# Cross-attention and expert layer on one core: second half ranked on shifted logits beside the exponentials, weight rows split behind their transposition, first-layer weights split in three portions

## The reference

```python
x = x + _L0_xattn_ref(_layernorm(x), ctx_768, Wq, Wk, Wv, Wo, bo)   # 8 heads of 64
x = x + _L0_ffn_ref(_layernorm(x), router_w, ...)

router_logits = flat @ router_w + router_b            # 1024 tokens x 8 experts
router_probs = jax.nn.softmax(router_logits, axis=-1)
topk_probs, topk_idx = jax.lax.top_k(router_probs, 2)
weights = jnp.zeros_like(router_probs).at[jnp.arange(T)[:, None], topk_idx].add(topk_probs)
shared_out = gelu(flat @ sw1 + sb1) @ sw2 + sb2
h1 = gelu(jnp.einsum('td,edh->teh', flat, rw1) + rb1)  # every expert, 256 wide
expert_out = jnp.einsum('teh,ehd->ted', h1, rw2) + rb2
mixed = jnp.einsum('ted,te->td', expert_out, weights)
```

## Time and profile before

| | |
|---|---|
| device time, median of 3 runs | 435.71 us (435.40 to 437.55) |
| device time of the profiled execution | 435.49 us |
| span of its profile | 433.7 us |
| mean granted TensorE clock | 0.992 of full |
| busy: PE / PEld / DVE | 420.8 / 327.0 / 278.3 us |
| busy: ACT / POOL | 219.3 / 257.8 us |
| chain that ended last: PE / POOL / DVE / ACT | 83% / 8% / 3% / 2% |

### The profile page before, as it was taken

One profiled execution on the slowest core, in us unless ns is written; L12 is line 12 of the kernel. 1 busy time (PEld: TensorE's weight loads), 2 busy tenths in 40 slices (PEclk: granted clock), 3 DMA queues, 4 the chain that ended last, 5 costly groups with the idle time before them and its releaser, 6 DMA issues.

```text
span 433.7 us, 7166 instructions
## 1 busy us (share of the span) xinstructions
PE 420.8 (97%) x2500; PEld 327.0 (75%) x2500; DVE 278.3 (64%) x553; ACT 219.3 (51%) x384; POOL 257.8 (59%) x176
## 2 busy tenths in 40 slices
PE   8999999999999999999999999999999999878997
PEld 6787777786877877777878786778686776756896
DVE  4785858785546858673458596743495865656553
ACT  3555353342763534336735353447244754883783
POOL 4628995868474849382757483917352900873981
PEclk9999999999999999999999999999999999997999
DMA  7400002000000020000000300000000032003200
GB/s 227 139 1 2 0 2 59 0 2 0 2 0 2 2 58 2 0 2 0 2 2 0 110 2 2 2 1 0 2 2 2 2 97 79 19 1 112 85 26 24
DMA packets 16329, 11.59 MB, mean 27 GB/s; under 512 B 9580, under 2 KB 13208, under 8 KB 16296
## 3 DMA queue, kind: packets, MB, share of 16 engines
q1 hardware_dynamic: 16296, 11.15, 9.5%
HBM read 10.55 MB, written 0.56 MB: 26 GB/s over the span
## 4 chain that ended last, share of the span: by engine, by line
PE 83%; POOL 8%; DVE 3%; ACT 2%; issue 1%; DMA 1%; SPq 1%; POOLq 0%; ACTq 0%
PE ps L1254 19%; PE ps L1238 10%; PE ps L1174 10%; PE ps L1239 10%; PE ps L1240 10%; PE ps L1086 7%; PE ps L1088 7%; PE ps L1087 7%; POOL work L559 4%; PE ps L1128 2%; PE ps L1186 1%; POOL g_lo L773 1%; DMA probs<-in_L_xattn_Wv_dram 1%; POOL w_lo L757 1%; POOL work L557 1%
## 5 line engine op out<-in xcount | busy, mean ns | idle before, releaser
L849 ACT ACTIVATE probs<-ps 128x512 f32<-128x512 f32 (+1 forms) x208 | 123.8, 598 | 134.8 <-PE ps L1240 127.8
L970 DVE TENSOR_REDUCE maxes<-ps 128x1 f32<-128x402 f32 x256 | 131.6, 567 | 55.4 <-PE ps L1174 55.3
L559 POOL TENSOR_TENSOR work<-work,probs 128x1024 f32<-128x1024 f32 x54 | 128.9, 2388 | 15.9 <-ACT probs L849 13.0
L1254 PE MATMUL ps<-probs,v_sb 128*64 128x256 f32 (+1 forms) x832 | 93.4, 381 | 0.0
L1254 PEld LDWEIGHTS ps<-probs,v_sb 128*64 128x64 f32 (+1 forms) x832 | 58.3, 137 | 33.9 <-ACT probs L849 3.7
L1238 PE MATMUL ps<-g_hi,ctxT_hi 97*128 97x512 f32 (+1 forms) x208 | 82.9, 399 | 0.0
L557 POOL TENSOR_TENSOR work<-probs 128x1024 f32<-128x1024 f32 x14 | 33.5, 2392 | 82.0 <-issue 61.6
L1239 PE MATMUL ps<-g_lo,ctxT_hi 96*128 96x512 f32 (+1 forms) x208 | 82.0, 394 | 0.0
L1240 PE MATMUL ps<-g_hi,ctxT_lo 96*128 96x512 f32 (+1 forms) x208 | 81.7, 393 | 0.0
L1174 PE MATMUL ps<-ctxT_hi,g_hi 96*128 96x402 f32 x256 | 72.6, 356 | 0.7 <-ACT ctxT_hi L788 0.4
L773 POOL TENSOR_TENSOR g_lo<-probs,g_hi 128x512 fp32r<-128x512 f32 x32 | 40.5, 1290 | 35.1 <-ACT g_hi L871 35.1
(11 more groups left out here) (147 smaller groups left out, 526.4 us busy)
## 6 DMA issues: line engine op xcount, KB each, us to landing
v_sb<-weight_rows SPq DMA_DIRECT2D x12, 256.0 KB, 4.0
raw<-in_ctx_T_dram SPq DMA_DIRECT2D x3, 600.4 KB, 4.5
work<-in_L_ffn_rw_dram SPq DMA_DIRECT2D x1, 1024.0 KB, 7.5
raw<-weight_rows SPq DMA_DIRECT2D x4, 256.0 KB, 3.6
g_hi<-neg_row SPq DMA_DIRECT2D x60, 0.5 KB, 2.0
raw<-in_ctx_T_dram SPq DMA_DIRECT2D x3, 150.8 KB, 2.8
x_sb<-in_x_dram SPq DMA_DIRECT2D x1, 384.0 KB, 5.6
early<-in_WqkT_dram SPq DMA_DIRECT2D x1, 336.0 KB, 5.1
```

The costliest lines, as they stand in the source:

```text
L559: ops.tensor_tensor(acc, acc, pr, ALU.add).then_inc(summed, 1)
L849: nc.scalar.activation(probs[0:rows, n % SLOTS, j, :], s_bank(chunk_no(*w))[0:rows, :], ACT.Exp, scale=SCALE).then_inc(probs_ready, 1)
L970: v.tensor_reduce(maxes[:, p % 2, i * T + t, blk:blk + 1], src[:, 0:BW], AX.X, ALU.max).then_inc(ring_taken, 1)
L1254: ins = mm(o_bank[DH * i:DH * (i + 1), :], v_sb[0:rows, c, h * DH:(h + 1) * DH], probs[0:rows, n % SLOTS, j, i * S:(i + 1) * S], start=(c ...
```

## The change

- `plan_experts`: "xt" goes from turn 4 to turn 5, "router" and "exp" from turn 5 to turn 6, "rank" behind the seconds of turn 6, "wrow" behind the seconds of turn 7. The step "best" is gone in both halves.
- Ranking no longer waits for exponentials: `mark_best` finds the two largest of the shifted logits (maximum 0; filler 1.0) and makes a mask of them. In the last half it follows the router directly on DVE; in the first half it stays at "rank". Then, with the exponentials: masked product, sum, reciprocal, and one product that writes the weights in all four row groups of `wrow`.
- Both halves now subtract the maximum on DVE and take one exponential instruction. In the last half exponentials and masked ones lie in PSUM (bank `O_BANK`).
- The split into high and low part of the weight rows is made after the transposition: `wT` gets the rounded copy, and eight of its rows then the difference (one more DVE instruction).
- First-layer weights are split in portions of 3, 2 and 4 experts, after pairs (0, 0), (0, 2) and (0, 3); the bias addition on POOL moves from after (0, 3) to after (0, 2), before the second portion. The quotients of (0, 0), (0, 2) and (1, 0) wait for them.
- Start: ACT casts Wv after all four context blocks, POOL takes two low parts before that of Wv.

```diff
@@ plan @@
-              (n_units + 1, 3): [("rank",), ("best",)], (3, 6): [("ring", ("wrow",))]}
+              (n_units + 1, 3): [("rank",)], (3, 6): [("ring", ("wrow",))]}
-        main += [("w1", k) for k in range(2) if n == 2 * k] + followers(n, n_units)
+        main += [("w1", k) for k, at in enumerate((0, 2, 3)) if n == at] + followers(n, n_units)
@@ plan_experts @@
-    amid = {0: [("sums", last_pair), ("quotient", last_pair + (0,)), ("quotient", last_pair + (1,))], 2: [("ring", ("y", b))], 4: [("ring", ("xt", b))],
-            5: [("ring", ("router", last)), ("exp", last)], 6: [("rank", last), ("best", last)], 7: [("ring", ("wrow", last))]}
-    behind = {2: [("roots", b)], 3: [("norm", b)]}
+    amid = {0: [("sums", last_pair), ("quotient", last_pair + (0,)), ("quotient", last_pair + (1,))], 2: [("ring", ("y", b))], 5: [("ring", ("xt", b))],
+            6: [("ring", ("router", last)), ("exp", last)]}
+    behind = {2: [("roots", b)], 3: [("norm", b)], 6: [("rank", last)], 7: [("ring", ("wrow", last))]}
@@ build @@
-    W1_CUT = NE - PAIRS
+    W1_PARTS = (slice(0, PAIRS - 1), slice(PAIRS - 1, PAIRS + 1), slice(PAIRS + 1, NE))
+        lexp_bank, chosen_bank = (ps[:, O_BANK, i * TH * E:(i + 1) * TH * E].rearrange("p (t e) -> p t e", e=E)
+                                  for i in range(2))
+        def routing(w):
+            return (lexp_bank, chosen_bank) if w == NHALF - 1 else (lexp[:], chosen[:])
@@ gpsimd @@
             low_part(0, 0)
+            low_part(0, 1)
...
-            for i in range(1, BLOCKS):
+            for i in range(2, BLOCKS):
...
-            g.memset(rprob[:], -1.0).then_inc(consts_ready, 1)
+            g.memset(logit[:], 1.0).then_inc(consts_ready, 1)
...
-                if kind == "scores" and w == (0, 3, NU - 1, 0):
-
-                    added(0, 3)
+                if kind == "w1" and w == 1:
+
+                    added(0, 2)
...
-                    es = (slice(0, W1_CUT), slice(W1_CUT, NE))[w]
+                    es = W1_PARTS[w]
-                    added(0, 2 * w)
+                    added(0, (0, 2, 3)[w])
@@ scalar @@
             for i in range(BLOCKS):
                 high_part(0, i)
-                if i == 1:
-                    act.wait_ge(s_wv, 16)
-                    nc.scalar.copy(wv_hi[:], wv_sb).then_inc(wv_hi_ready, 1)
+            act.wait_ge(s_wv, 16)
+            nc.scalar.copy(wv_hi[:], wv_sb).then_inc(wv_hi_ready, 1)
...
+                    nc.scalar.activation(routing(w)[0], logit[:, :, 0:E], ACT.Exp).then_inc(lexp_ready, 1)
@@ vector @@
-                if p == 0 and b < 2:
-                    dve.wait_ge(w1_split, b + 1)
+                if (b, p) in ((0, 0), (0, 2), (1, 0)):
+                    dve.wait_ge(w1_split, ((0, 0), (0, 2), (1, 0)).index((b, p)) + 1)
+            def mark_best(w):
+                dve.wait_ge(logit_ready, w + 1)
+                for t in range(TH):
+                    ins = v.max(top8[:, t, :], logit[:, t, 0:E])
+                then_own(ins)
+                then_own(v.memset(top8[:, :, TOP:8], 1.0))
+                for t in range(TH):
+                    ins = v.match_replace(low[:, t, 0:E + 8 - TOP], top8[:, t, :], logit[:, t, 0:E + 8 - TOP], 1.0)
+                then_own(ins)
+                then_own(v.tensor_scalar(mask[:], low[:, :, 0:E], 0.5, None, ALU.is_gt))
...
+                        then_own(v.tensor_reduce(neg_lmax[:], lg, AX.X, ALU.max, negate=True))
+                        v.tensor_tensor(lg, lg, neg_lmax[:].unsqueeze(2).to_broadcast([P, TH, E]), ALU.add
+                        if b == NHALF - 1:
+                            mark_best(b)
...
-                        v.tensor_copy(wT[:, b * HALF:(b + 1) * HALF], src).then_inc(ring_taken, 1)
+                        cols = slice(b * HALF, (b + 1) * HALF)
+                        then_own(v.tensor_copy(wT[:, cols], src))
+                        v.tensor_tensor(wT[WLO:WLO + E, cols], src[WLO:WLO + E, :], wT[WLO:WLO + E, cols].bitcast(F32),
+                                        ALU.subtract).then_inc(ring_taken, 1)
                 elif kind == "rank":
+                    le, ch = routing(w)
+                    if w < NHALF - 1:
+                        mark_best(w)
                     dve.wait_ge(lexp_ready, w + 1)
+                    v.tensor_tensor(ch, le, mask[:], ALU.mult)
+                    then_own(v.tensor_reduce(lsum[:], le, AX.X, ALU.add))
                     then_own(v.reciprocal(rsum[:], lsum[:]))
...
+                    v.tensor_tensor(wr, ch.unsqueeze(2).to_broadcast([P, TH, P // WLO, E]),
+                                    rsum[:].unsqueeze(2).unsqueeze(3).to_broadcast([P, TH, P // WLO, E]), ALU.mult
+                                    ).then_inc(w_ready, 1)
```

More of the change, by code:

```diff
@@ L380, in build @@
         w_rows = sb("w_rows", [P, NHALF, HALF])
-        logit = sb("logit", [P, TH, E])
+        logit = sb("logit", [P, TH, E + 8])
+        mask = sb("mask", [P, TH, E])
         neg_lmax = sb("neg_lmax", [P, TH])
@@ L852, in _ @@
                     act.wait_ge(logit_ready, w + 1)
-                    if w == NHALF - 1:
-                        nc.scalar.activation(lexp[:], logit[:], ACT.Exp).then_inc(lexp_ready, 1)
-                        continue
-                    for t in range(TH):
-                        ins = nc.scalar.activation(lexp[:, t, :], logit[:, t, :], ACT.Exp,
-                                                   bias=neg_lmax[:, t:t + 1])
-                    ins.then_inc(lexp_ready, 1)
+                    nc.scalar.activation(routing(w)[0], logit[:, :, 0:E], ACT.Exp).then_inc(lexp_ready, 1)
                 elif kind == "split":
@@ L1017, in _ @@
+                    if w < NHALF - 1:
+                        mark_best(w)
                     dve.wait_ge(lexp_ready, w + 1)
-                    then_own(v.tensor_reduce(lsum[:], lexp[:], AX.X, ALU.add))
+                    v.tensor_tensor(ch, le, mask[:], ALU.mult)
+                    then_own(v.tensor_reduce(lsum[:], le, AX.X, ALU.add))
                     then_own(v.reciprocal(rsum[:], lsum[:]))
                     if w == 0:
-                        dve.wait_ge(consts_ready, 3)
-                    else:
-                        dve.wait_ge(w_ready, w)
@@ L1025, in _ @@
-                    then_own(v.tensor_tensor(rprob[:, :, 0:E], lexp[:], rsum[:].unsqueeze(2).to_broadcast([P, TH, E]),
-                                             ALU.mult))
-                    for t in range(TH):
-                        ins = v.max(top8[:, t, :], rprob[:, t, 0:E])
-                    then_own(ins)
-                    then_own(v.memset(top8[:, :, TOP:8], -1.0))
-                    for t in range(TH):
-                        ins = v.match_replace(low[:, t, 0:E + 8 - TOP], top8[:, t, :], rprob[:, t, 0:E + 8 - TOP], 0.0)
@@ L1033, in _ @@
-                    ins.then_inc(ranked, 1)
-                elif kind == "best" and w == NHALF - 1:
-                    dve.wait_ge(ranked, w + 1)
-                    dve.wait_ge(wrow_zero, 2)
-                    wr = wrow[:, w * TH:(w + 1) * TH, :]
-                    weight = wr[:, :, W4:W4 + E]
-                    then_own(v.tensor_tensor(weight, rprob[:, :, 0:E], low[:, :, 0:E], ALU.subtract))
-                    then_own(v.tensor_copy(w_hi[:], weight))
-                    hi = w_hi[:].bitcast(F32)
-                    v.tensor_copy(*high_weights(wr))
-                    v.tensor_tensor(wr[:, :, WLO:WLO + E], weight, hi, ALU.subtract).then_inc(w_ready, 1)
+                        dve.wait_ge(wrow_zero, 2)
```

20 lines of the change are left out of this document (8 added, 12 removed).

## The result

The changed kernel took 431.67 us (median of 4 runs, 430.69 to 433.09) against 436.63 us (4 runs) for the kernel before on the same chip: a ratio of 0.9904 [0.9877, 0.993], faster by 1.0%. The sign of the forecast held; the size did not: 428.9 us was forecast, with a range up to 431.4. The profiled execution took 430.69 us (span 428.6), 4.8 us less than the profiled one before; its three companions took up to 2.4 us more. So there are two misses to explain: 1.8 us in the profiled execution, and 1 us or more between it and the others.

A forecast was written before the change was run, and what follows sets the result against it. TensorE, busy for 97% of the span, was taken to bound the kernel, so only its waits matter. The terms summed to 435.49 - 7.8 - 0.9 + 2.1 = 428.9 us, range 426.3 to 431.4.

The forecast's parts named there:

- Bound and places: Whole kernel: TensorE busy for 97% of the span, about 9.2 us to be had from its waits and fallen clock.
- The three waits named: TensorE's waits: 5.0 us for the second half's ranking, 1.5 us for `xn`, 0.8 us for the second head pair's sums.
- The start: Kernel start: moving the Wv cast behind all four context casts costs 0 (-0.2 to +0.5).
- Second half, -7.8: Expert stage: moved steps make weight rows ready before TensorE asks, the clock never falls there; -7.8 us (-6.6 to -8.4).
- The router's wait: Second half: a new TensorE wait before the second router, 0.6 to 1.1 us, taken as 0.8.
- Spread of the rows: Behind the second transposition: DVE waits up to 2.4 us for SP's spread; TensorE has about 1 us of cover.
- First weights, -0.9: Near 65 us: three portions let POOL add the second pair's probabilities earlier, ending TensorE's 0.8 us wait; -0.9 us.
- First half, +2.1: DVE near 254 us: the new shift waits for POOL's running addition, delaying TensorE; +2.1 us (0 to +2.4).
- (a): First half: the shift is not blocked or its delay is absorbed; 426.8 us, chance 0.2.
- (b): Second half: ranking late again, by a blocked shift or waits for rows or spread DMA; 430.0 to 431.5 us, chance 0.18.
- (c): Second half: weighings ahead on DVE set the ranking's end and the clock falls again; 433 to 434.5 us, chance 0.04.
- (d): First half: DVE's mask, product and weights each blocked 2.4 us beside POOL's additions; 436.1 us, slower, chance 0.02.

The follow-up runs named there:

- e9: e6 with the second half's exponentials and masked ones in SBUF instead of PSUM: 428.71 us, ratio 0.9831.
- e7: The kernel before with only the three-portion split of first weights and the moved bias addition: 435.43 us, ratio 0.9991.
- e8: The changed kernel with 12 small filler products on TensorE before the maximum it waits for in the first half: 430.87 us, ratio 0.989.
- e1: The changed kernel with the first half's logits left in PSUM, so the shift has one SBUF input: 427.30 us, ratio 0.9809.
- e10: The changed kernel unaltered, ten further executions on another chip: 432.37 us, ratio 0.9935.
- e4: e1 with the second half's exponentials and masked ones in SBUF instead of PSUM: 428.19 us, one execution.
- e5: e3 with one more reduction on DVE that lengthens TensorE's wait: 432.20 us, ratio 0.9907.
- e11: e1 again, unaltered, on another chip: 429.89 us, ratio 0.9858.
- e2: The changed kernel with 20 small filler products on TensorE before the maximum it waits for in the first half: 429.79 us, ratio 0.9849.
- e3: e1 with a useless DVE sum of two SBUF tiles added in pair (1, 2), far from any router: 429.36 us, ratio 0.9847.
- e12: e6 again, unaltered, on another chip: 426.77 us, ratio 0.9792.
- e6: e1 with `xt` split before the weighings of the expert stage's sixth turn on DVE: 427.34 us, ratio 0.9807.

## Why the prediction was right or wrong

- **Bound and places**: right. The three waits named went, and the time came from there. The start cost nothing, as forecast (the gap of PE near 25 us stands behind 24.80, before 24.84).
- **Second half, -7.8**: right, 7.73 measured up to item 16 and 0.16 behind it (the forecast's own parts, 7.7 and 0.2, add up to 7.9). Taking off the 2.80 us by which the stage began late: rows ready at 387.4 (forecast 387.4), PE at 387.8 (387.8), item 16 at 388.2 (388.2), the mask 0.88 us (0.9), shift and masked product unblocked at 0.19 and 0.20. The router's wait was 0.56 in place of 0.8. The shift has two SBUF inputs here as in the first half; it was free because POOL stood still (386.74 to 387.99). e9 shows that PSUM was the reason for the unblocked product: it takes 1.22 us from SBUF.
- **Spread of the rows**: right as far as seen. DVE is idle for 1.92 us before the weighing at 397.14 (the profile names no releaser for it), and PE does not wait.
- **First weights, -0.9**: right in the changed kernel, where 0.87 us stand behind the third pair and 0.84 at the router. As a gain of its own it is within the noise of e7's times, and in e7's profile the clock took it back behind 392 us.
- **First half, +2.1**: the step that failed. The blocked operation and PE's delay were as forecast (2.12 us; 2.2 at the value products of e8, where the clock stayed up), and e1 shows the cause by taking it away. But the term counted only the wait. Of the 5 us wait of the second half I had counted 1.8 us of clock; of a wait of 1.6 us none, and gave no reason. The trace before does hold a row for it, which I didn't use: the wait of 1.51 us for `xn` before 377.35 went by at clock 1.00 (window as in the earlier trace rows):

```profile
364.00:384.00 20.00, 18.49 (x99) 14.53 (x94) 11.08 (x24) 15.38 (x27) 12.03 (x13) 1.00 0.16 52
```

So it was open which way a wait of 1.6 us would go, and the upper end of the term had to hold the clock. The term should have been 3.6 (the first profile) to 5.0 (e10: 1.4 more, with 6.8 us at half clock). With 3.6 the sum is 435.49 - 7.8 - 0.9 + 3.6 = 430.4, against 430.69 measured. Why a wait of 1.59 us was followed by a fall and one of 1.51 was not stays open.
- **The rest of the median**: 1.0 us, open. The changed kernel's other runs had 0.990 to 0.992 against 0.996 of the profiled one, so they lost more clock. One place for it is the second router: I forecast that wait and counted 0.8 us for it, not the fall behind it, which the profiles of e1, e4, e5, e10 and e11 show (3.4 us at half clock) and those of e2, e3, e8 and the first of the changed kernel don't. The other is a longer fall in the first half, as in e10. Which of them each run had was not seen, since they have no trace; nor is it known whether they had the later start of the last section.
- **Rivals**: (a) was not what happened, but it is e1: 427.30 measured against 426.8. (b) named the time of the profiled execution, 430.0 to 431.5, for a wrong reason; (c) and (d) did not occur: DVE's mask and product of the first half took 0.18 and 0.19 us (267.95 and 268.17), with POOL idle.
- **The page on table loads**: the Trainium skill, "ScalarE: Activation LUTs" (What ACT_TABLE_LOAD costs), gave 2.66 us with the drain. Here the load at 388.45 took 1.28 and the Gelu stood at 389.75; the load for the exponential (385.53 to 386.81) was through before the logits were there (387.14). The measurement decides, and by it nothing waits.
- **The page on memory**: "SBUF — State Buffer" of the Trainium skill (Who interferes with whom) held in every case made here: 2.12, 1.95, 1.21 and 1.22 us beside POOL with both inputs in SBUF, 0.19 and 0.20 with one in PSUM, and 0.19 with both in SBUF and POOL idle.

## What to carry to other kernels

Price a new wait of TensorE with its clock, also if it is under 2 us, at least as the upper end of a range: here a wait of 1.6 us took 1.5 to 2.8 us more behind it, and filler products in the gap, or taking the wait away, kept the clock at 1.00 at that place. The length alone does not decide: waits of 1.51 us (kernel before, e7), 1.24 (e3) and 1.04 (e9) went by without a fall. Before a small VectorE operation is put beside a stream of GpSimd additions, look where its inputs lie; leaving one of them in PSUM made 2.12 us into 0.19. And a small gain ahead of a place where the clock falls can be given back there, in one profile whole (e7), so remove the large wait first. The kernel with both remedies, e12, takes 426.77 us: 0.9792 [0.9755, 0.9829] of before, and 1.3% under the changed kernel on the same chip.

## What the runs showed of the hardware that was not expected

- The same code with the same wait lost the full clock for 3.4 us in one execution (258.6) and for 6.8 in another (259.6). In the 5 us wait of the kernel before and of e7 the fall came 2.5 us behind the last product ahead of the wait in the first and 4.3 us behind it in the second; in e7 it so reached 2.3 us into item 16 and what follows it, before only 0.5.
- Behind a wait of 0.56 us just ahead of the router's twelve narrow matmuls the clock fell in five profiles of nine that have it (e1, e4, e5, e10, e11; not in e2, e3, e8 and the first of the changed kernel); with the wait gone, the narrow matmuls alone had no fall in the profiles of e6, e9 and e12, and e6 and e12 kept 1.0 in all eight executions. What decides between the nine is not known.
- The start has two lengths: the gap of PE near 25 us stood at 24.4 to 24.8 us in some executions and at 25.8 to 26.3 in others, of the same code (e6 26.02, e12 24.69). In the latter the 256-column matmuls at 7.7 us have a pitch of 0.21 us, in the former of 0.12: the full clock comes later. These 1.0 to 1.9 us can be in any comparison of two single runs.
